# Audio tower on one core: last batch in smaller pieces, bias rows by ScalarE, gamma and beta spread by a matmul

## The reference, cut to what matters

```python
# token mixer
x_sp  = depthwise_conv3(x, conv_w) + conv_b
mixed = einsum('btc,dc->btd', x_sp^T, lin_w) + lin_b + emb.mean(axis=0)
h     = (mixed - mean) * rsqrt(var + 1e-5) * ln_g + ln_b
# attention on n1 = layernorm(h)
QK = (n1 Wq)(n1 Wk)^T ; A = softmax(QK / 8)
A[row c0] = 0, with c0 = argmin of batch 0's row sums of QK
h  = h + A (n1 Wv)
# feed-forward on n2 = layernorm(h), W1 and W2 lower triangular
h  = h + (gelu(n2 tril(W1)^T + b1) tril(W2)^T + b2)
```

## Time and profile before

| | us |
|---|---|
| runs of before | 95.37, 94.71, 94.94 (median 94.94) |
| the profiled execution | 94.69 |
| its span, first to last instruction | 92.9 |
| TensorE busy | 87.2 |
| VectorE / ScalarE / GpSimd busy | 74.4 / 69.3 / 47.8 |
| granted TensorE clock | 1.00 of full speed throughout |

### The profile page before, as it was taken

How to read it: one execution, slowest core, us unless ns; L and a number is a source line. 1 busy time by engine, 2 the same in 40 slices (tenths; PEclk the granted TensorE clock), 3 DMA queues, 4 the chain that set the end, 5 groups by cost and what they waited for, 6 DMA issues and landing times.

```text
span 92.9 us, 2013 instructions
## 1 busy us (share of the span) xinstructions
PE 87.2 (94%) x567; PEld 73.9 (80%) x567; DVE 74.4 (80%) x296; ACT 69.3 (75%) x215; POOL 47.8 (51%) x70
## 2 busy tenths in 40 slices
PE   4999699999999999999999999999999999999940
PEld 1356567789999999999999999999997877787840
DVE  3279997999698998869998895988989688793560
ACT  1666799899999969977889976697758983565200
POOL 7006398676554386539525519703996305791000
PEclk9999999999999999999999999999999999999999
DMA  2896000000000000000000000000000003036565
GB/s 17 213 280 212 0 0 4 4 0 0 7 0 0 0 0 0 7 4 0 0 4 4 0 7 0 0 0 0 0 0 7 0 0 110 0 110 169 162 175 167
DMA packets 3973, 3.86 MB, mean 42 GB/s; under 512 B 429, under 2 KB 3962, under 8 KB 3962
## 3 DMA queue, kind: packets, MB, share of 16 engines
q1 hardware_dynamic: 3610, 3.35, 12.8%
q10 hardware_dynamic: 352, 0.38, 1.5%
HBM read 1.68 MB, written 2.05 MB: 40 GB/s over the span
## 4 chain that ended last, share of the span: by engine, by line
PE 80%; DVE 9%; DMA 5%; issue 1%; SPq 0%; DVEq 0%
PE bank_o L483 15%; PE bank_s L458 15%; PE bank_at L470 8%; PE bank_pv L434 7%; PE bank_pv L443 7%; PE bank_s L518 7%; DMA x_all<-x_dram 5%; PE bank_x L366 4%; PE bank_x L496 4%; PE bank_nt L507 4%; PE bank_pv L507 4%; PE bank_nt L423 4%; DVE hb_all L1078 2%; DVE tap_a L994 1%; DVE xc L1000 1%; PE bank_o L366 1%
## 5 line engine op out<-in xcount | busy, mean ns | idle before, releaser
L483 PE MATMUL bank_o<-pv,at_sb 125*125 125x129 f32 x128 | 16.8, 273 | 0.0
L458 PE MATMUL bank_s<-n1t,pv 128*125 128x250 f32 x64 | 16.1, 374 | 0.0
L483 PEld LDWEIGHTS bank_o<-pv,at_sb 125*125 125x125 f32 x128 | 15.6, 187 | 0.1
L772 ACT ACTIVATE a<-bank_s,neg_max 125x250 f32<-125x250 f32 x32 | 13.4, 482 | 1.0 <-DVE neg_max L1039 1.0
L1039 DVE TENSOR_REDUCE neg_max<-bank_s 125x2 f32<-125x500 f32 x16 | 10.7, 668 | 2.2 <-PE bank_s L458 2.1
L458 PEld LDWEIGHTS bank_s<-n1t,pv 128*125 128x125 f32 x64 | 11.0, 187 | 0.9
L780 ACT ACTIVATE at_sb<-bank_at 125x500 f32<-125x500 f32 x16 | 9.6, 597 | 2.4 <-PE bank_at L470 1.8
L276 POOL TENSOR_TENSOR hb_all<-h_all,rows_sb 125x512 f32<-125x512 f32 x8 | 10.9, 1384 | 0.0
L765 ACT ACTIVATE pv<-bank_pv 128x508 f32<-128x508 f32 x15 | 9.0, 602 | 2.1 <-PE bank_pv L443 2.0
L272 POOL TENSOR_TENSOR h_all<-h_all,rows_sb 125x512 f32<-125x512 f32 x6 | 7.6, 1271 | 5.7 <-DVE h_all L1013 5.7
L1050 DVE SCALAR_TENSOR_TENSOR h_all<-bank_o,rinv_keep,h_all 125x128 f32<-125x128 f32 x32 | 9.8, 346 | 0.6
(11 more groups left out here) (137 smaller groups left out, 183.7 us busy)
## 6 DMA issues: line engine op xcount, KB each, us to landing
out_dram<-hb_all SPq DMA_DIRECT2D x7, 224.0 KB
x_all<-x_dram SPq DMA_DIRECT2D x8, 125.0 KB, 4.9
out_dram<-hb_all SPq DMA_DIRECT2D x2, 112.0 KB
w_sb<-weights_dram SPq DMA_DIRECT2D x1, 192.0 KB, 5.6
rows_sb<-rows_dram ACTq DMA_DIRECT2D x1, 187.5 KB
out_dram<-hb_all SPq DMA_DIRECT2D x6, 26.0 KB
tok_w<-tok_dram ACTq DMA_DIRECT2D x1, 130.0 KB, 3.1
w_sb<-weights_dram SPq DMA_DIRECT2D x1, 128.5 KB, 5.2
```

The lines of the kernel that those rows point to most:

```text
L458: last = nc.tensor.matmul(s_ps[b % 2][:, a, :], p_sb(b)[:, a * H:(a + 1) * H], n1t[b % 2][:, :], start=True, stop=True)
L483: last = nc.tensor.matmul(o_ps[:, a, 0:DV], at_sb[:, c, a * H:(a + 1) * H], v_sb(b, c), start=(c == 0), stop=(c == 1))
L772: last = nc.scalar.activation(a_sb[b % 2][:, a, :], s_ps[b % 2][:, a, :], ACT.Exp, bias=neg_max[b % 2][:, a:a + 1])
```

## The change

- `rows_sb` is no longer loaded: one row of 1 KB lands in `rows_raw` (zeroed by GpSimd first), a matmul with `mean_w` (1/64 on 64 rows) spreads it over 125 rows, ScalarE copies it out times 64. b2 has its own load, issued by SyncE behind all of x.
- The bias row is copied out of PSUM by ScalarE (`out_cb`) and split into bf16 parts by four GpSimd operations that stand before and behind `head_root_x(0, 1, 2)`. Only pairs 2 and 3 use the bf16 product; for pairs 4 to 7 ScalarE writes the row into the bank (`write_bias`).
- The first tap of pair 1 goes from VectorE to ScalarE; ScalarE has both first taps (1 and 2) before `squares(0)`.
- Pair 7 is taken in two turns of one batch each (`turn`) from the second root to the last `down`; the last batch's two tiles go to two banks, are added by 128 columns each, and stored in three transfers, two of them of 512 bytes a row.
- `keep_warm` 9 to 6, and every queue's list is in a new order.

```diff
-        y_last = [bank_s[1][0:H, 0:2 * D].rearrange("p (n d) -> p n d", d=D),
-                  bank_at[0:H, 0:2 * D].rearrange("p (n d) -> p n d", d=D)]
+        y_last = [t[0:H, 0:D] for t in (bank_at, bank_o)]
...
+        def turn(j):
+            return (j, 0, 4, 2 * j + 2) if j < NP - 1 else (NP - 1, 2 * (j - NP + 1), 2, j + NP)
...
+            sp.dma_start(b2_sb[:, :], rows[:, 2 * D:3 * D].broadcast_to((H, D))).then_inc(landed_b2, 16)
...
-            for b in (0, 1):
-                sp.wait_ge(y_ready, NP + b)
-                sp.dma_start(out_pairs[NP - 1][0:WIDE, b], hb_rows[0:WIDE, NP - 1, b]).then_inc(out_done, 16)
+            sp.wait_ge(y_ready, NP + 1)
+            sp.dma_start(out_pairs[NP - 1][0:WIDE, 1, 0:D], hb_rows[0:WIDE, NP - 1, 1, 0:D]).then_inc(out_done, 16)
+            sp.wait_ge(y_ready, NP + 2)
+            sp.dma_start(out_pairs[NP - 1][WIDE:H, 1], hb_rows[WIDE:H, NP - 1, 1]).then_inc(out_done, 16)
...
+            def split_hi():
+                pool.wait_ge(cb_out, 1)
+                pool.tensor_copy(cb_rows[:, :], cb_sb[:, :]).then_inc(cb_hi_ready, 1)
+            def split_rest():
+                pool.wait_ge(cb_hi_ready, 1)
+                pool.tensor_tensor(cb_rest[:, :], cb_sb[0:64, :], cb_rows[0:64, :], ALU.subtract).then_inc(cb_rest_ready, 1)
+            def split_mid():
+                pool.wait_ge(cb_rest_ready, 1)
+                pool.tensor_copy(cb_rows[0:64, :], cb_rest[:, :]).then_inc(cb_mid_ready, 1)
+            def split_low():
+                pool.wait_ge(cb_mid_ready, 1)
+                pool.tensor_tensor(cb_rows[0:32, :], cb_rest[0:32, :], cb_rows[0:32, :], ALU.subtract)\
+                    .then_inc(cb_ready, 1)
...
             head_root_x(0, 0, 2)
+            split_hi()
+            split_rest()
             head_root_x(0, 1, 2)
+            split_mid()
+            split_low()
             head_root_1(0)
...
+            def spread_constants():
+                pe.wait_ge(mean_w_ready, 2)
+                pe.wait_ge(landed_rows, 16)
+                nc.tensor.matmul(bank_at[0:H, 0:2 * D], mean_w[:, 0:H], rows_raw[:, :], start=True, stop=True).then_inc(rows_mm, 1)
...
-            keep_warm(9)
+            keep_warm(6)
+            spread_constants()
             project_first(0)
+            qk_product()
...
+            def write_bias(k):
+                act.wait_ge(cb_out, 1)
+                act.wait_ge(conv_ready, k + 1)
+                nc.scalar.activation(x_bank(k)[0:H, :].rearrange("p (a d) -> p a d", d=D),
+                                     cb_sb[0:H, :].unsqueeze(1).broadcast_to((H, 4, D)), ACT.Copy).then_inc(bias_ready, 1)
```

More of the change, by code:

```diff
@@ L494, in turn_n2 @@
                     pe.wait_ge(n2t_ready, j - 1)
-                for n in range(4):
-                    last = nc.tensor.transpose(t2_ps[j % 2][:, n * H:(n + 1) * H], n2[:, j, n, :], ident[0:H, 0:H])
+                k, first, count, _ = turn(j)
+                for n in range(count):
+                    last = nc.tensor.transpose(t2_ps[j % 2][:, n * H:(n + 1) * H], n2[:, k, first + n, :], ident[0:H, 0:H])
                 last.then_inc(t2_mm, 1)
@@ L603, in _ @@
             values(8)
-            project_bias(7)
+            attend(5)
             project_half(7, 0)
             project_half(7, 1)
+            queries(9)
+            turn_a(6)
             scores(8)
-            attend(5)
-            turn_a(6)
-            queries(9)
             turn_n1(10)
+            w1_centre()
             values(9)
@@ L802, in _ @@
                                      bias=neg_mean[half, 1:2]).then_inc(lin_ready, 1)
+            first_tap(1)
+            first_tap(2)
             squares(0)
+            out_qk(0)
+            out_cb()
+            out_constants()
             squares(1)
-            first_tap(2)
-            out_qk(0)
             first_tap(3)
             squares(2)
+            squares(3)
+            out_wv()
             out_qk(1)
-            squares(3)
-            out_qk(2)
             normalize_1(0)
-            out_wv()
             squares(4)
@@ L816, in _ @@
             out_n1t(0)
+            out_qk(2)
+            spread_rows()
             normalize_1(1)
-            spread_rows()
             out_p0()
-            first_tap(4)
             squares(6)
             out_n1t(1)
-            squares(7)
+            first_tap(4)
             out_v0()
@@ L826, in _ @@
             out_pv(1)
+            squares(7)
+            write_bias(4)
+            out_n1t(2)
             first_tap(5)
-            out_n1t(2)
-            squares(8)
             normalize_1(3)
@@ L898, in _ @@
             normalize_1(15)
+            out_at(11)
+            out_w1()
             exps(12)
             out_pv(14)
-            out_at(11)
-            out_w1()
+            out_at(12)
+            exps(13)
             out_n1t(15)
-            exps(13)
-            out_at(12)
             out_n2t(0)
             exps(14)
+            out_at(13)
             out_pv(15)
-            out_at(13)
+            gelu(0)
+            out_at(14)
             exps(15)
             out_n2t(1)
-            out_at(14)
@@ L913, in _ @@
-            gelu(0)
             out_n2t(2)
+            gelu(1)
+            gelu(2)
+            out_at(15)
             out_n2t(3)
-            gelu(1)
-            out_at(15)
-            gelu(2)
             out_n2t(4)
             gelu(3)
+            gelu(4)
             out_n2t(5)
             out_n2t(6)
-            gelu(4)
             gelu(5)
+            gelu(6)
             out_n2t(7)
-            gelu(6)
+            out_n2t(8)
             gelu(7)
+            gelu(8)
             act.wait_ge(y_ready, NP - 1)
@@ L1169, in _ @@
             gather_1(11)
-            row_max(7)
-            residual(4)
-            scale_x(12)
-            moments_2(2)
-            scale_x(13)
-            gather_2(0)
-            gather_2(1)
-            moments_2(3)
+            third_tap(7)
+            moments_2(1)
+            residual(4)
+            moments_2(2)
+            row_max(6)
+            scale_x(12)
+            scale_x(13)
+            moments_2(3)
+            row_max(7)
+            moments_2(4)
             residual(5)
```

495 lines of the change are left out of this document (245 added, 250 removed).

## The result

The changed kernel took 95.86 us (median of 8 runs; 94.82 for the kernel before beside it). The ratio is 1.0088, with a 95% interval from 1.0049 to 1.0128: about 0.8 us slower, where 0.33 us less was forecast. The profiled execution took 95.59 us with a span of 93.8, 0.9 more than before.

A forecast was written before the change was run, and what follows sets the result against it. TensorE was taken as the bound, with ScalarE also full from 13.9 to 31.6 us. Terms -0.25 - 0.44 + 0.36 = -0.33 us, on the median of 94.94 us, gave 94.6 us; 8-in-10 range 93.1 to 96.0.

The forecast's parts named there:

- The price of the tail: Last batch at the end: half turns, waits, adds and store issues sum to +0.36 us, bounds -0.3 and +0.8.
- The wait ahead of down(7): TensorE near the end: it stands until 1.16 us after up(7) starts, because the first Gelu ends only at 1.10.
- The -0.1 us of a smaller last transfer: End of the kernel: the last transfer is half as large, worth about -0.1 us.
- the start: Up to queries(0): lightening VectorE by some 1.9 us is worth 0.12 us, as GpSimd and ScalarE are late next.
- the landing: Start: pair 2's data taken to land at 5.8 us, bounds 5.1 and 7.7; rival of 7.7 us, chance 0.08.
- The new matmul over gamma and beta: Warm-up on TensorE: some 0.45 us, costing nothing if its 1 KB lands by 4.5 us, up to 0.4 if not.
- the last root: GpSimd at the start: the root batch 0's first normalisation waits for runs from 10.99 to 11.97 us.
- The full stage: Up to 31.6 us, ScalarE full: of 0.74 us gained 0.49 are given back, leaving -0.25; attend(2) at 31.3.
- The ScalarE walk: From out_n1t(0) to out_pv(5): ScalarE's work grows from 17.67 to 18.5 us, so out_pv(5) starts at 32.15 at best.
- The bias matmuls of pairs 6 and 7: Behind 31.6 us: ScalarE has room, so taking these matmuls off TensorE brings -0.44 us.
- The stage at 54 to 63 us: Middle of the kernel: the prediction did not look at this stage and its sum has no term for it.
- The table loads: ScalarE, Gelu ahead of the last Exp: two more loads, 2.57 us, are covered and cost nothing; uncovered rival, chance 0.15.

The follow-up runs named there:

- b_128: Kernel before with the store part alone: last batch's two tiles in two banks, two adds of 128 columns, five stores for the last pair; ratio 1.0051.
- a_first: Changed kernel with the start's small operations reordered and pair 2's bias from the full-precision product, so only pair 3 waits for GpSimd's split; ratio 1.0058.
- a_root2: Changed kernel with the root of batches 14 and 15 ahead of the second root on GpSimd, and normalize_2(0) moved later on VectorE; ratio 1.0068.
- a_mix2: Changed kernel with both reorderings, a_first and a_root2; ratio 1.003 to the kernel before.
- a_bias_pe: Changed kernel with the bias of pairs 4 to 7 back on TensorE, ScalarE's four bias writes gone; ratio 1.0145 to the kernel before.
- a_warm9: Changed kernel with nine warm-up matmuls again instead of six; ratio 1.0176 to the kernel before.
- a_whole: Changed kernel with the last batch's end as before: one bank, one add and the kernel before's three stores; ratio 1.0081 to the kernel before.
- a_rows_dma: Changed kernel with gamma and beta spread by a transfer to 125 partitions again, as before; ratio 1.0469 to the kernel before.
- b_bias67: Kernel before with the bias of pairs 6 and 7 alone written by ScalarE; ratio 1.0035.

## Why the prediction was wrong

**The price of the tail was right** (+0.36 forecast, about +0.35 measured from up(7) on). The wait ahead of down(7) is there as worked out: down(7) starts 1.15 us behind up(7), 1.16 forecast. The last issue is 1.16 us behind the last pass (forecast 1.08). The -0.1 us of a smaller last transfer has no run behind it. From the last issue to the end it is 2.7 us here against 2.9 before, but 2.9 to 3.4 in b_128, a_first, a_root2, a_mix2, a_bias_pe and a_warm9 with the same small transfer: that this term came out was luck. And b_128 and a_whole do not agree on what the store part costs, so the sum is right and its parts are only in part shown. One reading of the working is wrong without a part in the sum: the last add of the kernel before ends 0.69 us behind the last pass (89.95 against 89.26), not 0.79.

**The first step that failed is the start**, "The whole lightening of VectorE (some 1.9 us) is thus worth 0.12 us". It cost 0.39 us at queries(0). The prediction had named GpSimd as next in line and had its splits right (0.29, 0.42, 0.28 and 0.42 us against 0.3 and 0.45), and pair 2 landed early enough: the tap of pair 2 ran straight behind that of pair 1 (5.8 us was taken for the landing). The Trainium skill, DMA: Bandwidth & Descriptors (Why a DMA increments its semaphore by 16 and not by 1), had led to an estimate of 6.4. The tap started at about 6.0, so that was a little late. Its rule has no row of its own here; a_rows_dma agrees in direction, as the broadcast alone brings the landing back to about 7.0. Two terms were mis-sized. The new matmul over gamma and beta was put at nothing if its row landed by 4.5 us; it started at 4.04, straight behind the warm-up, and with slow matmuls squares(0) came 0.33 us later than forecast, of which 0.19 were left at the end of the split (11.18 against 10.99). And the last root, from there to its end, took 1.26 us (0.98 forecast), because its small addition stood beside VectorE (0.46 us for 0.20). That makes the 0.47 us at the first normalisation. The prediction gave GpSimd's chain no slack, rightly, but took its small addition at its undisturbed time. a_first and a_mix2 show that the loss need not come with the change: with the chain's operations ahead of the last split step, and pair 2 off the split, 0.4 to 0.6 us come back at attend(2).

**The full stage** had attend(2) at 31.3, and it came at 31.84. Of these 0.54 us, 0.47 are the start's. From the first normalisation to attend(2) 19.3 us were forecast and 19.37 measured, so this step was right: ScalarE is full (17.70 of 17.70), and a_bias_pe shows that what the moved bias rows of pairs 4 and 5 save on TensorE is all given back. The ScalarE walk was less exact than it looks: out_pv(5) came 19.87 us behind the first normalisation, 20.15 by the forecast, and its own terms add up to 18.6 us and not 18.5.

**The bias matmuls of pairs 6 and 7**, -0.44 us because "Behind 31.6 us ScalarE has room", were half right. They are gone from TensorE, but attend(2) takes 0.13 us longer in the kernel after than in a_bias_pe, and giving all four back costs only 0.22 us behind it. In the kernel before they are worth nothing: b_bias67 lost just as much TensorE time as it saved.

**The stage at 54 to 63 us** was not in the sum, and this is the second step that failed: its price was put at nothing without a reason. The rewritten order of roots and second normalisations was part of the change, and the prediction read it only at the start and at the end. It cost 0.59 us; a_root2 gets half of it back.

**The table loads were right**: covered, with three of them in the queue. The trace gives 1.28 us for the load at 71.71, and the Exp starts at 73.00. The Trainium skill, ScalarE: Activation LUTs (What ACT_TABLE_LOAD costs), gives the same for the load and about 1.38 us for a drain beside it, some 2.7 us a switch; the drain is not to be seen in this queue.

Together, against the forecast: the start and the stage up to attend(2) +0.54 us, attend(2) itself +0.13, the stage at 54 us +0.59, and no other term over 0.05. That is 1.26 us, where 1.2 lie between -0.33 and +0.9; the rest is in terms of a few hundredths.

## What to carry to other kernels

When a change rewrites the order of the queues, walk every queue from end to end for pairs of neighbours that changed places, not only the stages that the change is about: 0.6 us were lost at 55 us, where nobody had looked, half of it by one root ahead of another. Work moved to an engine with idle time is free only if it does not stand ahead of an operation of the chain that sets the end. And moving an operation means moving what waits for it in the other engine's queue too: one without the other cost 1.8 us, both together won 0.2 to 0.3. Before a gain is read off two profiles, subtract what their starts differ by: executions of one order differed by 0.45 us at the first normalisation (12.28 to 12.73).

## What the runs showed of the hardware that was not expected

- A GpSimd operation on 125 x 2 elements takes 0.20 us, and 0.46 or 0.80 when VectorE starts an operation with two SBUF inputs ahead of it; it ends about 0.05 us behind VectorE's.
- Issuing a store took 0.32 to 0.48 us as a rule, but single issues took 0.72 to 2.27 near the end, in eight kernels here, before and after alike. What decides it stays open; it moved the end by up to 1.3 us.
- In the kernel after and in a_whole the add behind the last passes starts 0.15 and 0.37 us behind the end of VectorE's add before it, although by their modelled ends the passes were over by then. The chain calls it issue; its cause was not found.
- ScalarE's copy of 508 columns grew in the kernel after, from 0.59 us at 18.0 to 0.75 at 28.8 and 0.84 at 35.3, while the engine had hardly a wait and the starts kept their spacing; at 38.8 it was 0.62 again. In a_bias_pe it stayed at 0.59 to 0.64. The copy that attend(2) waits for took 0.73 us in the first and 0.60 in the second, and attend(2) 1.02 and 0.89. The cause is open.
- The granted clock was 1.00 from 4 to 6 us while the two instructions of a 256-column fp32 matmul took 1.19 us, which took 0.59 in a_warm9 at the same granted clock. The clock's row does not show this loss.
